# A two-layer graph attention kernel: each kind of phase gets an order of stages of its own, and the adjacency is loaded between the copies of the stacks

## Reference

```python
# layer 0
scores = (x @ Wq + bq) @ (x @ Wk + bk).T / sqrt(256)
scores = where(adj == 0, -1e18, scores)
attn = where(adj == 0, 0, softmax(scores))
x = layer_norm(x + (attn @ x) @ Wc) * gamma + beta
# layer 1, 8 heads of 32 channels
logits = q_h @ k_h.T / sqrt(32) + log(clip(adj, 1e-8))
attn = softmax(logits)
x = layer_norm(x + concat_h(attn @ v_h) @ Wo.T + bo) * gamma + beta
```

## Time and profile before

| | us |
|---|---|
| runs, median of 3 | 1358.18 (1352.55 to 1370.64) |
| the profiled execution, its own time | 1355.97 |
| its span | 1354.0 |
| PE busy | 1194.5 (88%) |
| DVE busy | 1005.1 (74%) |
| POOL busy | 744.6 (55%) |
| ACT busy | 523.2 (39%) |

### The profile page before, as it was taken

One profiled execution on the slowest core, in us unless ns is written; L12 is line 12 of the kernel. 1 busy time (PEld: TensorE's weight loads), 2 busy tenths in 40 slices (PEclk: granted clock), 3 DMA queues, 4 the chain that ended last, 5 costly groups with the idle time before them and its releaser, 6 DMA issues.

```text
span 1354.0 us, 21123 instructions
## 1 busy us (share of the span) xinstructions
PE 1194.5 (88%) x6458; PEld 705.6 (52%) x6474; DVE 1005.1 (74%) x1744; ACT 523.2 (39%) x1004; POOL 744.6 (55%) x359
## 2 busy tenths in 40 slices
PE   6789889888998989899899989989898988989962
PEld 5555454545646455564545556454555545465511
DVE  4365877878687786868778787878878787777863
ACT  1224344434244433434444343434444334434331
POOL 0016458383564837465483846558384745738483
PEclk8879999999899999999999999999999989999876
DMA  3041231404213150412314041231404123140300
GB/s 117 0 119 38 59 98 45 128 16 113 58 48 107 35 136 16 120 51 60 95 41 130 16 126 45 63 92 48 123 16 131 40 62 93 51 120 16 91 18 15
DMA packets 69651, 94.66 MB, mean 70 GB/s; under 512 B 14081, under 2 KB 32769, under 8 KB 69634
## 3 DMA queue, kind: packets, MB, share of 16 engines
q1 hardware_dynamic: 69634, 94.44, 25.1%
HBM read 35.40 MB, written 8.39 MB: 32 GB/s over the span
## 4 chain that ended last, share of the span: by engine, by line
PE 35%; POOL 19%; SPq 14%; issue 12%; DVE 9%; DMA 6%; ACT 4%; POOLq 0%; DVEq 0%; ACTq 0%
SPq L408 13%; POOL PR L1104 10%; DMA ADJ<-adj_t 5%; PE misc L560 5%; PE misc L625 4%; PE values L703 4%; PE misc L612 3%; POOL z L1116 3%; POOL res L1089 3%; PE scores L681 3%; POOL res L1087 3%; PE misc L570 2%; DVE xn L1004 2%; PE denominators L703 2%; PE values L730 2%
## 5 line engine op out<-in xcount | busy, mean ns | idle before, releaser
L1104 POOL TENSOR_TENSOR PR<-PR,CLIP 128x1024 f32<-128x1024 f32 x224 | 540.4, 2429 | 503.0 <-ACT PR L807 503.0
L807 ACT ACTIVATE PR<-scores 128x512 f32<-128x512 f32 x512 | 278.0, 597 | 283.7 <-PE scores L681 280.2
L965 DVE TENSOR_REDUCE mx<-misc 128x1 f32<-128x512 f32 x512 | 320.5, 680 | 82.9 <-PE misc L660 80.3
L681 PE MATMUL scores<-QS,KS 97*128 97x512 f32 x512 | 200.6, 469 | 18.4 <-ACT PR L807 12.7
L703 PE MATMUL values<-PR,V 128*32 128x512 f32 x1024 | 143.7, 635 | 31.6 <-POOL PR L1104 31.6
L703 PE MATMUL denominators<-PR,ones 128*32 128x512 f32 x1024 | 144.7, 639 | 3.1 <-POOL PR L1104 3.1
L681 PEld LDWEIGHTS scores<-QS,KS 97*128 97x128 f32 x512 | 90.6, 200 | 108.1 <-ACT PR L807 61.4
L660 PE MATMUL misc<-K1H,Q1H 32*128 32x512 f32 x512 | 117.5, 501 | 8.6 <-DVE mx L965 3.4
L638 PE MATMUL misc<-U,P 128*128 128x257 f32 x512 | 122.2, 387 | 0.0
L1012 DVE RECIPROCAL sums_w<-sums_w 128x128 f32<-128x128 f32 x128 | 113.8, 923 | 6.0 <-ACT sums_w L817 6.0
L660 PEld LDWEIGHTS misc<-K1H,Q1H 32*128 32x128 f32 x512 | 49.8, 183 | 112.2 <-DVE mx L965 62.0
(11 more groups left out here) (159 smaller groups left out, 1997.7 us busy)
## 6 DMA issues: line engine op xcount, KB each, us to landing
ADJ<-adj_t SPq DMA_DIRECT2D x16, 1024.0 KB, 6.0
QS<-Q1H SPq DMA_DIRECT2D x256, 64.0 KB, 2.0
KS<-K1H SPq DMA_DIRECT2D x256, 64.0 KB, 2.0
P<-x_t SPq DMA_DIRECT2D x16, 512.0 KB, 3.8
X<-x SPq DMA_DIRECT2D x16, 512.0 KB, 3.7
QS<-Q1L SPq DMA_DIRECT2D x128, 64.0 KB, 2.0
KS<-K1L SPq DMA_DIRECT2D x128, 64.0 KB, 2.0
out<-z SPq DMA_DIRECT2D x16, 512.0 KB, 2.9
```

The costliest lines, as they stand in the source:

```text
L681: pe.matmul(ST[n][:], KS[:, h, P * k:P * (k + 1)], QS[:, h, :], start=True, stop=True).then_inc(scores_filled, 1)
L807: act.activation(PR[quad % WEIGHT_BUFFERS][:, h, :], ST[n][:], ACT.Exp, scale=SCALE1).then_inc(exp_done, 1)
L965: dve.tensor_reduce(mx1[:, g, h, t:t + 1], misc_bank(ph, "max1", g, n)[:], AX.X, ALU.max, negate=True).then_inc(misc_drained["dve"], 1)
L1104: pool.tensor_tensor(w, w, clipped, ALU.mult).then_inc(masked_pool, 1)
```

## The change

1. `SCHEDULE` is now the order of the mixed phases (and of the end), with a new order. The first phase gets `FIRST`, the last phase `LAST`. Whether VectorE does a mask is looked up by the kind of phase: in the last phase VectorE has nine of sixteen, (0,1), (3,0), (3,1), (4,0), (4,1), (5,0), (6,0), (7,0), (7,1); in the mixed ones (4,0) and (5,0) as before. The counts of semaphores follow from that.
2. SyncE loads the next adjacency after the first 12 copies to the stacks of group 0, behind a wait for CLIP. Before, the load stood behind all 24, and behind the row of maxima.

```diff
+ORDERS = {"first": FIRST, "steady": SCHEDULE, "last": LAST, "end": SCHEDULE}
+
+
+def dve_masks(kind):
+    return [s[1:] for s in ORDERS[kind] if s[0] == "mask"]
+
+
+def masks(ph, by_dve, quad):
+
+    n = sum(1 for q, _ in dve_masks(ph.kind) if q <= quad)
     return n if by_dve else 2 * quad + 2 - n
+
+
+def masks_before(ph, by_dve):
+
+    n = len(dve_masks("steady"))
+    return ph.i * (n if by_dve else 2 * QUADS_PER_GRAPH - n)
...
-    return [s for s in SCHEDULE if present(s)]
+    return [s for s in ORDERS[ph.kind] if present(s)]
...
+FIRST = [
+    ("split", 0), ("split", 1), ("bias",), ("q0", 0), ("q0", 1), ("u", 0), ("u", 1), ("u", 2), ("max0", 0),
...
+    ("scores0", 0), ("scores0", 1), ("prepare", 0), ("scores0", 2), ("scores0", 3), ("prepare", 1),
...
-            def load_stacks(g):
-
-                for h in range(PER_GROUP):
+            def load_stacks(g, heads=range(PER_GROUP)):
+
+                for h in heads:
...
-                load_stacks(0)
+                load_stacks(0, range(PER_GROUP // 2))
+                if ph.front:
+
+                    sp.wait_ge(adj_clipped, i + 1)
+                    load_adj(j)
+
+                load_stacks(0, range(PER_GROUP // 2, PER_GROUP))
                 sp.wait_ge(misc_drained["dve"], misc.count_before(ph, "mrow1", 0))
                 load_mrow(0)
-                if ph.front:
-
-                    sp.wait_ge(adj_clipped, i + 1)
-                    load_adj(j)
-
                 load_stacks(1)
...
-                    pe.wait_ge(masked_pool, ph.i * masks(False, QUADS - 1) + masks(False, quad))
-                    if any(q == quad for q, _ in DVE_MASKS):
-                        pe.wait_ge(masked_dve, ph.i * len(DVE_MASKS) + masks(True, quad))
+                    if masks(ph, False, quad) > (masks(ph, False, quad - 1) if quad else 0):
+                        pe.wait_ge(masked_pool, masks_before(ph, False) + masks(ph, False, quad))
+                    if any(q == quad for q, _ in dve_masks(ph.kind)):
+                        pe.wait_ge(masked_dve, masks_before(ph, True) + masks(ph, True, quad))
```

More of the change, by code:

```diff
@@ L57, in __init__ @@
         self.kind = ("steady" if self.front else "last") if self.back else ("first" if self.front else "end")
-SCHEDULE = [
-    ("split", 0), ("split", 1), ("reciprocal", 1, 0), ("reciprocal", 1, 1), ("max1", 1, 0), ("max1", 1, 1),
[13 rows of a table removed]
-    ("reciprocal", 0, 0), ("scores1", 6, 0), ("transpose", 0), ("transpose", 1), ("scores1", 6, 1),
-    ("reciprocal", 0, 1), ("reciprocal", 0, 2), ("reciprocal", 0, 3), ("values1", 5), ("prepare", 2),
[6 rows of a table removed]
-]
-DVE_MASKS = [s[1:] for s in SCHEDULE if s[0] == "mask"]
-def masks(by_dve, quad):
-    n = sum(1 for q, _ in DVE_MASKS if q <= quad)
+FIRST = [
[9 rows of a table added]
+]
+SCHEDULE = [
+    ("reciprocal", 1, 0), ("max1", 1, 0), ("split", 0), ("split", 1), ("reciprocal", 1, 1),
[13 rows of a table added]
+    ("reciprocal", 0, 0), ("reciprocal", 0, 1), ("scores1", 6, 0), ("transpose", 0), ("scores1", 6, 1),
+    ("transpose", 1), ("reciprocal", 0, 2), ("reciprocal", 0, 3), ("values1", 5), ("scores1", 7, 0),
[6 rows of a table added]
+]
+LAST = [
+    ("max1", 1, 0), ("reciprocal", 1, 0), ("reciprocal", 1, 1), ("reciprocal", 1, 2), ("scores1", 0, 0),
[8 rows of a table added]
+    ("mask", 4, 1), ("mask", 5, 0), ("denominators1", 3), ("sums_out", 0), ("scores1", 6, 0),
[3 rows of a table added]
+    ("high_output", 0), ("denominators1", 7), ("mask", 7, 1), ("values1", 7), ("normalise", 0),
+    ("sums_out", 1), ("low_output", 0),
+]
+ORDERS = {"first": FIRST, "steady": SCHEDULE, "last": LAST, "end": SCHEDULE}
[3 more added lines that the diff above has]
+    n = sum(1 for q, _ in dve_masks(ph.kind) if q <= quad)
     return n if by_dve else 2 * quad + 2 - n
+def masks_before(ph, by_dve):
+    n = len(dve_masks("steady"))
+    return ph.i * (n if by_dve else 2 * QUADS_PER_GRAPH - n)
 MISC_BANKS = 4
@@ L121, in present @@
         if stage[0] == "prepare":
-            return ph.kind == "first"
+            return True
         return ph.tail if is_tail(stage) else ph.back if is_back(stage) else ph.front
-    return [s for s in SCHEDULE if present(s)]
+    return [s for s in ORDERS[ph.kind] if present(s)]
 class MiscBanks:
@@ L135, in __init__ @@
         assert all(len(self.uses[k]) % MISC_BANKS == 0 for k in ("first", "steady"))
-        assert self._last("first") == self._last("steady")
+        assert all(MISC_DRAIN[s[0]] for k in ("first", "steady") for s in self.uses[k][-MISC_BANKS:])
         self.graphs = graphs
-    def _last(self, kind):
-        uses = self.uses[kind]
-        return [next(s for s in uses[-1 - n::-MISC_BANKS] if MISC_DRAIN[s[0]]) for n in range(MISC_BANKS)]
     @staticmethod
@@ L160, in count, with _kind_before @@
         return self._base(ph, what) + self._number(uses[: uses.index(stage) + 1], what)
+    @staticmethod
+    def _kind_before(ph):
+        return "steady" if ph.tail else "first"
     def count_before(self, ph, *stage):
-        uses, e = self.uses["steady"], MISC_DRAIN[stage[0]]
-        later = [s for s in uses[uses.index(stage) + 1:] if MISC_DRAIN[s[0]] == e]
-        assert not any(map(is_back, later))
-        return self._base(ph, e) - self._number(later, e)
+        uses, e = self.uses[self._kind_before(ph)], MISC_DRAIN[stage[0]]
+        return self._base(ph, e) - self._number(uses[uses.index(stage) + 1:], e)
     def before(self, ph, *stage):
@@ L705, in sums1, with values_first @@
                 return mm
-            def values_first(quad):
-                return SCHEDULE.index(("values1", quad)) < SCHEDULE.index(("denominators1", quad))
+            def values_first(ph, quad):
+                order = ORDERS[ph.kind]
+                return order.index(("values1", quad)) < order.index(("denominators1", quad))
             def values1(ph, quad):
-                first = values_first(quad)
+                first = values_first(ph, quad)
                 mm = sums1(ph, quad, PV, first)
@@ L716, in denominators1 @@
             def denominators1(ph, quad):
-                first = not values_first(quad)
+                first = not values_first(ph, quad)
                 mm = sums1(ph, quad, DEN, first)
@@ L911, in wait_high @@
             def wait_high(ph, stage, c):
-                nth = [s for s in SCHEDULE if s[0] in SPLIT].index((stage, c))
+                nth = [s for s in ORDERS[ph.kind] if s[0] in SPLIT].index((stage, c))
                 dve.wait_ge(hi_written, ph.j * (C * len(SPLIT)) + nth + 1)
@@ L930, in clip @@
                 if ph.back:
-                    dve.wait_ge(masked_pool, (ph.i + 1) * masks(False, QUADS - 1))
+                    dve.wait_ge(masked_pool, masks_before(ph, False) + masks(ph, False, QUADS - 1))
                 dve.tensor_scalar(CLIP[:], ADJ[:], ADJ_MIN, None, ALU.max).then_inc(adj_clipped, 1)
@@ L1097, in mask @@
             def mask(ph, quad, pair):
-                if (quad, pair) in DVE_MASKS:
+                if (quad, pair) in dve_masks(ph.kind):
                     return
```

7 lines of the change are left out of this document (4 added, 3 removed), and 56 rows, old and new, of tables (FIRST, LAST, SCHEDULE).

## The result

The changed kernel takes 1314.14 us, median of 4 runs (1312.98 to 1315.61). The kernel before took 1360.1 us, median of 4 (1352.55 to 1370.64). The ratio is 0.9657, with a 95% interval of 0.959 to 0.9724. So it is 3.4% faster, inside the range given (1264 to 1330), but 21 us above the 1293 of the forecast and 2 us outside that case's own range.

What follows compares the result with a forecast made beforehand. TensorE was taken to stand waiting in each pass, mainly for a late ABSENT before max0. Loop -46, mixed phase before it -1.5, first phase -6, last -11 sum to -64.5 us: 1293 us, 8-in-10 range 1264 to 1330.

Steps and rivals of the forecast that it cites:

- the forecast: Main case: the loop's stall before max0 goes and both end phases gain; 1293 us, own range 1275 to 1312, chance 0.64.
- rival 1: The loop's stall moves: ABSENT's wait goes, but xn and XTL take back most; 1320 us, chance 0.20.
- Segment B: Loop pass, first scores to first scores0 product: TensorE's waits and the reduced clock go; -4.5 us, bounds -2.7 and -4.8.
- Segment A: Loop pass, q1 to first scores: XTL, behind one more reciprocal and maximum, delays q0; +1.0 us, bounds 0 and +1.2.
- Segment C: Loop pass, on to the end of the fourth context0: quad 3's denominators, eight matmuls, move behind it; -1.0 us.
- 0 taken, +0.5 as bound: Same stretch up to the fourth context0: GpSimd's residual ahead of mask (3,1) costs nothing, at most +0.5 us.
- Segment D: Loop pass, fourth context0 to next q1: the chain through xn stays and q1 follows xn later; +1.2 us, bound -0.8.
- what is late next is xn: Before the next q1: with TensorE's mask wait mostly filled, the chain statistics, rstd, xn does not shorten.
- First phase: Stretch before the loop: earlier ABSENT and U groups end the shift's wait at 30.4; -6 us, bounds -3 and -7.
- Last phase: After the loop: seven masks moved from GpSimd to VectorE shorten the line of masks; -11 us, bounds -7 and -14.
- 18 in all: Quad 4's first scores to the copy of the sums: masks 12.7 us, sums and exponentials some 5; 27.3 before.
- The end phase keeps its 24 us: From the last copy of the sums to the kernel's end: order and 24 us unchanged, change 0.

Runs made afterwards that it cites:

- e9: The kernel before with only the adjacency's new, earlier place on SyncE: 1347.5 us, ratio 0.9894 to the kernel before.
- e1: Changed kernel with the adjacency issued behind the row of maxima again: 1342.1 us, ratio 0.988 to the kernel before.
- e5: Changed kernel with XT's two splits ahead of the reciprocal and the maximum again in the mixed phase: 1325.9 us, 11.7 over the changed kernel.
- e7: Changed kernel with the second mask of quad 5 on VectorE behind xn instead of on GpSimd, in the mixed phase: 1285.1 us, 29.0 under the changed kernel.
- e8: Changed kernel with the last phase's masks, on both engines, multiplying 8 of 512 columns only: 1311.4 us, 2.8 under the changed kernel.
- e10: Changed kernel with 8 and 13 unread matmuls on TensorE ahead of quads 0 and 4 of the last phase: 1311.1 us, 3.0 under the changed kernel.
- e6: Changed kernel with the denominators of quad 3 ahead of the scores of quad 5 in the mixed phase: 1303.0 us, 11.1 under the changed kernel.

## Why the prediction was right, and where it was not

**Which case.** Faster by over 2% was right. The named mechanism of the forecast, the stall at max0, went as told. But the time is closer to rival 1 (1320) than to the forecast (1293), and by the segments it is neither. Rival 1 wanted the reduced clock behind max0 to stay at least in part (B -2.7, or half of it regained), and it went; that xn and XTL would take back much of the gain, as rival 1 has it, came true for XTL.

**Segment B (-4.5; measured -4.2).** Right. ABSENT starts with no DMA to wait for and TensorE comes to it on time. e9 and e1 add what the prediction didn't see: the adjacency and the order each buy little alone (1.1% and 0.2%), and the margin is nearly nothing. e5 and e1 show that a wait of 0.9 us for ABSENT made B 2.3 longer.

**Segment A (+1.0; measured +1.9).** Undersized. XTL ends later and q0 waits, as told (0.47 us, plus 0.26 for XTH), and e5 measures that at 1.5 us a pass rather than 1.0. The rest is the clock, which the prediction took to be cured with B's stall: it falls behind the new wait for xn in every second pass (25.5 against 24.3 us).

**Segment C (-1.0; measured 0.0).** The step that failed is "0 taken, +0.5 as bound" for mask (3,1). TensorE has eight matmuls fewer there, but waits 0.72 us for that mask, which stands behind the residual on GpSimd, and 0.26 us for an exponential: 0.98 us.

**Segment D (+1.2; measured +0.8 between undisturbed passes, 10.04 and 10.84, and +0.3 on the mean).** Right in kind: "what is late next is xn" held, and the reason it was late could have been priced. The prediction saw xn at 1.38 and at 3.43 us and put that down as a bound of one segment. e7 shows it was the largest term open: 26 us in the mixed phases (29 by the medians). In the trace it looks like a lock: GpSimd's mask starts 0.77 us after xn's first operation, and xn's fourth, begun during the mask, takes 2.45 us, to 0.15 us past the mask's end. The Trainium skill, page "SBUF — State Buffer", section "Who interferes with whom", says that VectorE's tensor_scalar can enter a mode in which it takes the port pair that it shares with GpSimd, and that the later of the two then blocks entirely. The trace agrees with the blocking: one wide SBUF input, 2.45 us beside a mask, 0.41 without; whether xn is in that mode no run here shows. The prediction had used that page only for operations with two SBUF inputs.

**First phase (-6; measured -5.6).** The sum was near by luck; its main step was wrong: the wait for the shift ends at 33.48, not 30.4 (before 35.23), so 1.8 us came of the 4.8. q0 begins 1.0 us later (19.46, before 18.48), since the first weights landed 1.2 us later (7.84 against 6.67), and three U groups behind it, the first still at the reduced clock, end at 27.27, where max0 starts. The rest is nearly all clock, which the prediction had as "some". The first half of the weights' preparation now lies between the scores0 products, and its second half starts 0.9 us earlier (43.96 against 44.86). TensorE does that half at its upper level after the change, and before at the lower one (before, then after):

```profile
44.86:51.41 6.55, 6.55 (x14) 3.92 (x14) 3.92 (x10) 2.19 (x4) 0.00 (x0) 0.53 0.00 1
```

```profile
43.96:47.56 3.60, 3.60 (x15) 2.37 (x14) 2.36 (x4) 2.66 (x5) 0.00 (x0) 1.00 0.00 0
```

That makes 3.9 us by the first context0 (47.56 against 51.41). The context0 products, at a clock of 1.00 against 0.78, give the rest: 7.2 us against 9.2. As the old order took from 67.8 to 73.3 us in three traces, the size of this term is not settled.

**Last phase (-11; measured -7.4, and -8.5 to -10.4 in the seven other kernels with the same last phase).** The 2 us ahead of quad 4 came (1.8). The term mis-sized is "18 in all" from quad 4 to the copy of the sums: 21.7. It was walked along the masks; once seven of them are off GpSimd, TensorE's own work is the line, and at the lower clock it takes longer than the 18 us walked. e8 takes the masks away and gains 0.7 us there; e10 takes the low clock away and reaches 17.1, near the 18 forecast, though by another path. "The end phase keeps its 24 us" missed by 1.1 in this execution, where the project's matmuls ran at the reduced clock throughout; in the seven others it is 23.95 to 24.4.

**What would show it.** ABSENT without a DMA wait, no wait before max0 and a clock of 1.00 behind it, XTL late and xn waited for: all there. Of VectorE's nine masks in the last phase only one takes over 2 us, 3.16 beside GpSimd's residual; the other eight take 1.16 to 1.77, since few of them now meet a GpSimd operation. The pass is 76.8 us, not 75.0, and the last phase 21.7, not 18.

## What to carry to other kernels

When a stall is removed from a pipeline of several engines, don't add its length to the gain before you have asked which engine arrives next, and with what margin: here two edits were worth 1.1% and 0.2% alone and 2.4% together, and curing a wait of 0.7 us (e5) cost 12 us. Where a duration comes in two sizes in one trace, as xn at 0.41 and 2.45 us per operation, look for a collision before calling it noise: find what runs beside the slow one, and move that. And a gain of the expected size doesn't show the expected cause: in e6 the wait that was to go had doubled.
